# Scaling x by D on ScalarE at the preparation, and adding the product to y with transposes on PE

## The reference, cut to what matters

```python
x = _silu(conv + conv_b)                       # [batch, l, 1024]
delta = softplus(x @ W_delta_1 @ W_delta_2 + b_delta_2)
Bm = x @ W_B
Cm = x @ W_C
h = h * exp(delta * A) + (delta * x) * B       # a scan over l, for each of 1024 x 16 states
y = einsum('ben,bn->be', h, Cm)
y_apply_D = y + x * W_D
y_skip = y_apply_D * _silu(skip)
return resid + y_skip @ W_out
```

## Time and profile before

| what | value |
|---|---|
| time, median of 3 runs | 2184.91 us (2182.64 to 2185.52) |
| the profiled execution | 2178.91 us |
| its span | 2177.1 us |
| mean granted TensorE clock | 0.961 |
| busy: PE, PEld | 1893.4 us (87%), 1585.3 us (73%) |
| busy: POOL | 1859.3 us (85%) |
| busy: DVE, ACT | 1726.6 us (79%), 1716.2 us (79%) |
| L1175, the matmuls with D | 512 records, 71.5 us busy |

### The profile page before, as it was taken

One profiled execution on the slowest core, in us unless ns is written; L12 is line 12 of the kernel. 1 busy time (PEld: TensorE's weight loads), 2 busy tenths in 40 slices (PEclk: granted clock), 3 DMA queues, 4 the chain that ended last, 5 costly groups with the idle time before them and its releaser, 6 DMA issues.

```text
span 2177.1 us, 35466 instructions
## 1 busy us (share of the span) xinstructions
PE 1893.4 (87%) x12005; PEld 1585.3 (73%) x12005; DVE 1726.6 (79%) x2529; ACT 1716.2 (79%) x3404; POOL 1859.3 (85%) x1256
## 2 busy tenths in 40 slices
PE   5677777999999998999999898999989898989883
PEld 4566767878787786878778786978778686767551
DVE  3487878898898989888888988888898978888332
ACT  3489797979888897979889897988889798888221
POOL 1299999899999999999999999999989899999312
PEclk9999898999999999999999999999999999999995
DMA  5656566765766575765756585765757464645310
GB/s 174 209 189 212 184 212 206 241 215 190 242 201 223 170 265 175 245 220 184 253 177 228 186 269 177 226 227 183 250 162 250 149 229 166 218 151 184 116 49 20
DMA packets 234672, 425.92 MB, mean 196 GB/s; under 512 B 18623, under 2 KB 134907, under 8 KB 234491
## 3 DMA queue, kind: packets, MB, share of 16 engines
q1 hardware_dynamic: 234490, 423.65, 59.0%
HBM read 339.18 MB, written 84.41 MB: 195 GB/s over the span
## 4 chain that ended last, share of the span: by engine, by line
PE 31%; POOL 16%; DVE 15%; ACT 10%; issue 7%; DMA 7%; DVEq 0%; SPq 0%; POOLq 0%; ACTq 0%
DVE h L971 10%; POOL hc L613 9%; PE mixed L1363 6%; PE bank L1152 6%; PE y_sum L1157 6%; PE pair_bank L1283 4%; DMA c_all<-bc_dram 4%; ACT u_t L747 3%; PE routed L1337 3%; POOL operand L597 2%; DVE hv L1034 2%; ACT operand L728 2%; DMA dx_q<-dx_dram 2%; PE routed L1237 1%; DMA dx_dram<-dx 1%
## 5 line engine op out<-in xcount | busy, mean ns | idle before, releaser
L613 POOL TENSOR_TENSOR hc<-h,c_all 128x1024 f32<-128x1024 f32 x512 | 1205.0, 2367 | 83.0 <-DVE h L971 76.0
L971 DVE TENSOR_TENSOR_SCAN h<-operand,carry,bank 128x512 f32<-128x512 f32 x528 | 649.2, 1266 | 126.1 <-PE bank L1152 112.7
L747 ACT ACTIVATE u_t<-dx_t,lbc 128x256 f32<-128x256 f32 x1408 | 631.8, 498 | 19.0 <-PE bank L1152 18.9
L1157 PE MATMUL y_sum<-ident,hc 128*128 128x128 f32 x4096 | 601.6, 278 | 7.5 <-POOL hc L613 6.8
L1152 PE MATMUL bank<-ident,u_t 128*128 128x128 f32 x2816 | 448.6, 284 | 165.5 <-DVE h L971 162.6
L1152 PEld LDWEIGHTS bank<-ident,u_t 128*128 128x128 f32 x2816 | 336.3, 145 | 274.1 <-issue 176.3
L1157 PEld LDWEIGHTS y_sum<-ident,hc 128*128 128x128 f32 x4096 | 490.7, 144 | 47.1 <-issue 27.5
L728 ACT ACTIVATE operand<-delta_q,neg_a 128x512 f32<-128x512 f32 x704 | 480.0, 711 | 0.0
L597 POOL TENSOR_TENSOR operand<-dx_q,b_all 128x1024 f32<-128x1024 f32 x160 | 378.4, 2365 | 8.4 <-DMA b_all<-bc_dram 8.4
L728 ACT ACTIVATE bank<-delta_q,neg_a 128x512 f32<-128x512 f32 x320 | 218.1, 682 | 204.1 <-DVE h L971 203.7
L971 DVE TENSOR_TENSOR_SCAN h<-bank,carry,operand 128x512 f32<-128x512 f32 x240 | 295.8, 1268 | 27.4 <-POOL operand L597 17.0
(11 more groups left out here) (119 smaller groups left out, 1858.5 us busy)
## 6 DMA issues: line engine op xcount, KB each, us to landing
c_all<-bc_dram SPq DMA_DIRECT2D x256, 512.0 KB, 4.3
b_all<-bc_dram SPq DMA_DIRECT2D x160, 256.0 KB, 5.5
win<-in_L_attn_W_in SPq DMA_DIRECT2D x64, 512.0 KB, 6.0
wskip<-in_L_attn_W_skip SPq DMA_DIRECT2D x64, 512.0 KB, 6.5
x_dram<-x SPq DMA_DIRECT2D x64, 256.0 KB, 6.2
delta_dram<-delta SPq DMA_DIRECT2D x32, 512.0 KB, 7.6
dx_dram<-dx SPq DMA_DIRECT2D x32, 512.0 KB, 5.3
delta_q<-delta_dram SPq DMA_DIRECT2D x32, 512.0 KB, 5.9
```

The source lines that it names most:

```text
L613: nc.gpsimd.tensor_tensor(hc[:, number % 3], h[:, number % 3], c_all[:, j % 2, s % 2:s % 2 + 1].to_broadcast([P, 2, SPAN]), ALU.mult).then ...
L747: last = nc.scalar.activation(u_t[:, j % 2, b], dx_t[:, k, b], ACT.Copy, scale=lbc[:, stage % 2, b, DELTA + n:DELTA + n + 1])
L971: nc.vector.tensor_tensor_scan(h[:, number % 3, q], first, second, start, ALU.mult, ALU.add).then_inc(scan_done.sem, 1)
L1157: return matmul(to, lhsT=of, rhs=ident[:], is_transpose=True, start=start, stop=stop, skip_group_check=True)
```

## The change

`diag_d` goes, with its eight ACT instructions ahead of the loop and PE's wait for them. A tile `xd` takes its place, two buffers of a pair. At slot TAPPED[p]+5 ACT multiplies the pair's x by D into `xd`, two instructions of 128x256 with a scale of one value for each partition. They wait for DVE's x and for the store that last read this buffer. SP at TAPPED[p]+6 stores `xd` in place of x. DVE, before it overwrites x, now waits for ACT's reads and not for the stores. PE's product with `diag_d` becomes four transposes for each pair, in the same form as those of L1157.

```diff
-        diag_d = sb("diag_d", P, ET, P)
-        x = sb("x", P, ET, T)
+        x, xd = sb("x", P, ET, T), sb("xd", P, 2, 2, T)
...
-                                        if v := due(sp, x_ready, t, p + 1):
-                                            sp.wait_ge(x_ready.sem, v)
+                                        if v := due(sp, xd_ready, t, p + 1):
+                                            sp.wait_ge(xd_ready.sem, v)
...
-                                        sp.dma_start(x_dram[side, :, 2 * p:2 * p + 2, part], x[:, 2 * p:2 * p + 2]).then_inc(
+                                        sp.dma_start(x_dram[side, :, 2 * p:2 * p + 2, part], xd[:, p % 2]).then_inc(
...
-                for et in range(ET):
-                    nc.scalar.activation(diag_d[:, et], ident[:], ACT.Copy,
-                                         scale=dskip[:, et:et + 1]).then_inc(diag_made, 1)
...
+                                for p in range(PAIRS):
+                                    if s == TAPPED[p] + 5:
+                                        if v := due(act, x_ready, t, p + 1):
+                                            act.wait_ge(x_ready.sem, v)
+                                        if v := due(act, x_stored[p % 2], t, p // 2):
+                                            act.wait_ge(x_stored[p % 2].sem, v)
+                                        for et in (2 * p, 2 * p + 1):
+                                            last = nc.scalar.activation(xd[:, p % 2, et % 2], x[:, et], ACT.Copy,
+                                                                        scale=dskip[:, et:et + 1])
+                                        last.then_inc(xd_ready.sem, 1)
...
-                                        for stored in x_stored:
-                                            if v := due(dve, stored, t - 1, 2):
-                                                dve.wait_ge(stored.sem, v)
+                                        if v := due(dve, xd_ready, t - 1, PAIRS):
+                                            dve.wait_ge(xd_ready.sem, v)
...
-                        if t == -FIRST and k == 0 and pair == 0:
-                            pe.wait_ge(diag_made, ET)
...
-                                last = matmul(y_sum[:, b, q * P:(q + 1) * P], lhsT=x_q[:, q, b * P:(b + 1) * P],
-                                              rhs=diag_d[:, 2 * quarter + q], start=b % 2 == 0 and q == 0,
-                                              stop=False, skip_group_check=True)
+                                last = add_turned(y_sum[:, b, q * P:(q + 1) * P], x_q[:, q, b * P:(b + 1) * P],
+                                                  b % 2 == 0 and q == 0, False)
```

More of the change, by code:

```diff
@@ L228, in build @@
         tail_ready, edge_ready = signal("tail_ready", "prep", PAIRS), signal("edge_ready", "prep", 1)
-        th_ready, x_ready = signal("th_ready", "prep", PAIRS), signal("x_ready", "prep", PAIRS)
+        th_ready, x_ready, xd_ready = (signal(n, "prep", PAIRS) for n in ("th_ready", "x_ready", "xd_ready"))
         lbc_done, lbc_ready = signal("lbc_done", "prep", 1), signal("lbc_ready", "prep", 1)
@@ L257, in build @@
         dve_chain, pool_chain = Chain(nc, stack, "dve_chain"), Chain(nc, stack, "pool_chain")
-        loads, a_ready, diag_made, ident_made, router_in, router_turned, vectors_ready, constants_made = (
+        loads, a_ready, ident_made, router_in, router_turned, vectors_ready, constants_made = (
             stack.enter_context(nc.semaphore(n)) for n in
-            ("loads", "a_ready", "diag_made", "ident_made", "router_in", "router_turned", "vectors_ready", "constants_made"))
+            ("loads", "a_ready", "ident_made", "router_in", "router_turned", "vectors_ready", "constants_made"))
         numbers = [s.sem.num for s in signals] + [s.num for s in (
-            dve_chain.sem, pool_chain.sem, loads, a_ready, diag_made, ident_made, router_in, router_turned, vectors_ready, constants_made)]
+            dve_chain.sem, pool_chain.sem, loads, a_ready, ident_made, router_in, router_turned, vectors_ready, constants_made)]
         router_rows = x1[0:EXPERTS, 0, :]
@@ L1164, in add_y @@
                     t, s = now
-                    _, quarter, n, k, number = place(t, s)
+                    _, _, n, k, number = place(t, s)
                     if n == 0:
-                        if t == -FIRST and k == 0 and pair == 0:
-                            pe.wait_ge(diag_made, ET)
                         if v := due(pe, xq_loaded, t, k + 1):
```

## The result

The changed kernel takes 2188.66 us (median of 20 runs, 2183.06 to 2191.38), the kernel before beside it 2182.85 us (20 runs, 2179.03 to 2189.69). The ratio is 1.0024, 95% interval 1.0015 to 1.0032: 5.2 us slower by the ratio, with 3.3 to 7.0 for the interval. The change costs about 6 us. The forecast, +2.7 us, had the right sign and half of the size, and its 2187.6 us stands as close to 2188.66 as it does because the three runs that it started from, 2184.91 us, lay some 2 us above the kernel's longer record. That closeness is luck.

The account below looks back on a forecast made before the run. No engine was solid; a chain of waits changing engines within each step was taken as the bound. Ramp +4.8, first steps +0.7, cover +0.5, PE -3.3 gave +2.7 us on 2184.91: 2187.6 us, range 2179 to 2200.

Parts of the forecast that it names:

- Ramp, +4.8: Two chunks prepared without a scan: ACT's wait for x and new work delay the serial loop 2.4 us each.
- The rival in which it is caught up: Steady part paced from elsewhere, so the ramp's 4.8 us vanish: 2182.8 us; chance 0.06.
- PE at slot 2, -3.3: Shorter PE groups at slot 2 save 3.3 us over 11 steps, limited by DVE's scan; bounds 0 and 12.
- the gain is 0.2: Turn of slot 5: PE 0.9 us sooner waits for DVE's scan, gaining 0.2 us in each of 8 steps.
- The steps sized at 0.45 and 0.8: Turn of slot 5: two steps gain 0.45 us each and one 0.8, the turn's distance behind its scan.
- PE in full: Rival: DVE's scan of slot 4 also comes sooner, PE saves 12 us instead of 3.3: 2178 us; chance 0.17.
- At slot 18 I count nothing: Slot 18: ACT or POOL holds the chain in nearly all steps, so PE's saving there counts 0.
- ACT beside the scan, +0.7 and +0.5: ACT's new instructions in scan steps cost 0.7 us in the first steps and 0.5 for all 56 pairs together.
- by a hair: Steady part: ACT's gaps hold the 0.8 us of each new pair, three of four only just.
- The rival of the short cover: ACT's gaps too short, one pair in each step pays 0.8 us, 11.2 in all: 2198.8 us; chance 0.22.
- SP's store of xd with the loads of C behind it: SP's queue: store reached after ACT, no cost; if it waited for ACT, loads of C and POOL would come later.
- The clock: Rival: transposes at slot 2 lower PE's granted clock in 12 steps, costing 24 us: 2211 us; chance 0.05.

Follow-up runs that it names:

- undoing PE's part: The changed kernel with ordinary fp32 matmuls by the identity in place of the new transposes; 1.0041 of the kernel before.
- the pair without the ramp's cost: Two changed kernels with xd behind hv of the next pair in scanless steps: with ordinary identity matmuls 1.0015, with transposes 1.0004 of the kernel before.
- PE's part alone: The kernel before with transposes of unscaled x at slots 2 and 18, no new ACT instructions, multiplication by D left out; 0.9995 and 0.9998.
- The doubled dose: The changed kernel with four more short ACT instructions for each pair in steps with a scan; 1.0043 of the kernel before.
- xd later in the ramp: The changed kernel with the new ACT instructions behind hv of the next pair in the two steps without a scan; 1.0004 of the kernel before.

## Why the prediction was half right

**Ramp, +4.8: right**, in its steps as in its sum. hv of pair 1 is 1.64 us later (forecast 1.6), that of pair 2 2.43 (2.4), the ramp is 4.9 us longer, and moving the instructions behind hv took it away. The rival in which it is caught up is refuted by the same run.

**PE at slot 2, -3.3: too large.** Measured alone, -0.8 us (between -2.2 and +0.7 by the two intervals together). With ACT's new work present, undoing PE's part cost 2.0 and 3.7 us against the two measurements of the changed kernel, and 2.4 us in the pair without the ramp's cost; their intervals are 2 us and more wide, so whether PE's saving is worth more when ACT is late is open. The mechanism was right: PE waits for DVE at the turn of slot 5, and the scan of slot 6 moves little. The step that failed is "the gain is 0.2", in the size of a term. It took the end of the scan as 960.4, with "an overlap of some 0.1" that isn't there for the last instruction: 958.01 + 2.45 is 960.46, the turn follows 0.05 us behind it, and a turn that had to wait passes on 0.05 us less than one that runs through. 0.06 us is left of 0.17. The steps sized at 0.45 and 0.8 gave 0.36 and 0.88, and two early steps that I had not singled out gave 0.86 each, so the sum at slot 6 is 3.8 us, near the forecast but from other parts. What failed for the total is that I took it as final: in PE's part alone some of it is gone at the end, and in the changed kernel two steady steps take 247.0 and 246.7 us in its two traces, against 246.9 in both of the kernel before and a forecast of 0.4 less (its 247.5 was one pair of steps, not their mean).

**PE in full: refuted** (12 us outside every interval). The chain passes through both groups of slot 2 in 12 steps, and more work there does cost 1.78 us in each steady step. But taking a piece off the chain is only worth its distance to the next-latest, and that is a tenth of a microsecond in most steady steps. "At slot 18 I count nothing" holds for taking away, where the wait for ACT's decay at slot 22 takes the 0.91 us back, and not for adding: there DVE's 0.47 us of waiting for ACT fill up first, and of 1.79 us at slot 21 1.24 reach slot 22 and 1.0 the end of the step.

**ACT beside the scan, +0.7 and +0.5: too small.** 3.3 us measured (1.3 to 5.2). The 0.5 us for the steady part were no worse than 0.4 off (0.1 to 0.2 read), but for the wrong reason: I matched each pair with the first gap behind it and found three of four "by a hair". The doubled dose shows that the gaps behind that one hold it as well. The rival of the short cover is refuted with it. The missing 2 us lie outside the steady part, so the term that failed is the 0.7 for the first steps, as far as is known: I had sized the shift by ACT's gaps and hidden half of it behind POOL's backlog. That all of the 2 us lie in those steps isn't shown, since what follows POOL's last product was about 1 us longer too. Nor is a second source excluded that I had put at nothing, SP's store of xd with the loads of C behind it. From the first scan to 2030 us POOL waits for these loads 3.1 to 10.9 us in all in the eight traces with xd, and 2.1 to 8.3 us in the six without.

**The clock: refuted where I put it.** At slot 2 of the changed kernel the granted clock stays at 1.00 (959 to 965 us). The rule of the Trainium skill (TensorE: Matmul & The Clock Gate, Part 4: PE-mode transpose) that transposes count less for the clock would have let it fall there. It did not, although PE ran transposes alone there from 959.01 to 961.66 us after a wait of 1.69 us; the matmuls of the output projection came right behind. It did fall at another place, in the 15th step, in both traces of the changed kernel:

```profile
1899.76 0.63 PE L1157 MATMUL bank<-ident,u_t 128*128 128x128 f32 x4 [2.05 <-DVE h L977]
1900.50 0.66 PE L1162 MATMUL y_sum<-ident,hc 128*128 128x128 f32 x4
1900.99 0.94 PE L1157 MATMUL bank<-ident,u_t 128*128 128x128 f32 x4
1901.72 1.06 PE L1162 MATMUL y_sum<-ident,hc 128*128 128x128 f32 x4
```

After a wait of 2.05 us with transposes alone behind it, four of them take 1.06 us, in place of 0.60. That step is 111.1 and 111.2 us long; before it was 108.7 and 109.1. The kernel with ACT's work doubled has it too (111.3), the other eleven traces have 108.3 to 109.3. So about 2 us of what the two traces of the changed kernel lost are this fall. What brings it about just there is open: no kernel isolates it. In the sum of the parts (4.9 + 3.3 - 0.8 = 7.4 us, against 5.2 and 7.0 measured) it has no term of its own, and none is missing within the intervals. My two mis-sized terms, by 2.5 us (PE) and 2.1 (ACT), erred to the same side; the start, 2.1 us too high, hid part of it.

**The best version** of those run is the one with xd later in the ramp, 1.0004 (0.9991 to 1.0016): no different from the kernel before. PE's part alone, without any of ACT's new work, is at 0.9995 and 0.9998. So even if ACT's work cost nothing, there would be some 0.8 us to gain, at most 2.2 by the intervals; none of the placements that were run made the kernel measurably faster.

## What to carry to other kernels

A piece of work on the chain of waits has two prices. Adding to it can cost its full length, as at slot 2; taking it away gains only the distance to the next-latest event, and later waits can still take that back, as ACT's decay did at slot 22. Read that distance to the hundredth, for each kind of step, before multiplying by a count. When an engine gets work, look first at the serial start-up phase: here 8 of the 64 new pairs of instructions cost 4.9 us and the other 56 cost 3.3. There the place in the stream decided: the same instructions behind the next pair's work cost nothing that could be measured. And take a second trace of the unchanged kernel before explaining a difference of a few microseconds between two traces; here it differed from the first by 4.7 us in one step.

## What the runs showed of the hardware

PE's granted clock can fall to 0.50 for some 3 us, in two cases some 7, after a wait of PE in the middle of dense work, in one execution of a program and not in another. The falls at the step ends came after waits of 1.9 to 3.7 us; waits of 0.5 to 2.3 us passed without one, so the length of the wait alone doesn't decide. And at the ramp's end the clock returned to 1.00 at anything from 0.1 us ahead of the start of the first scan to 2.8 us behind it (from the mean clock over stretches of 2 us), with the same kind of work ahead of it. In the kernel before (windows of PE, clock third from the end), then in the changed one:

```profile
111.18:113.18 2.00, 2.00 (x6) 0.50 0.45 179
113.18:115.18 2.00, 2.00 (x10) 0.83 0.74 247
...
115.41:117.41 2.00, 2.00 (x6) 0.50 0.34 132
117.41:119.41 2.00, 2.00 (x7) 0.51 0.82 261
119.41:121.41 2.00, 1.86 (x13) 1.00 1.01 387
```
